# First attention of a fused vision tower: images loaded once, two units beside each other in the row halves

## The reference

```python
patches = img.reshape(B, C, Hp, p, Wp, p).transpose(0, 2, 4, 1, 3, 5).reshape(B, S, C * p * p)
h = einsum('bsk,ek->bse', patches, w) + b            # p = 16, C = 3, k = 768, e = 128
h = h + L0_attn(layernorm(h))    # quantized q, k, v; causal softmax over 196 tokens
h = h + L0_ffn(layernorm(h))     # 8 experts, each takes its best 1024 tokens
h = h + L1_attn(layernorm(h))    # 8 heads, causal
h = h + L1_ffn(layernorm(h))     # 8 experts, two per token
```

## Time and profile before

| | |
|---|---|
| median of 3 runs | 1897.94 us (1896.28 to 1905.5) |
| profiled execution | 1896.8 us, its span 1895.0 us |
| mean granted TensorE clock | 0.929 |
| PE busy | 1663.5 us, 88% of the span |
| PEld busy | 1212.7 us, 64% |
| DVE busy | 1181.9 us, 62% |
| ACT busy | 1075.5 us, 57% |
| POOL busy | 1168.5 us, 62% |
| DMA moved | 172.42 MB, mean 91 GB/s |
| patch products, L449 | 512 matmuls, 207.0 us busy, 511 ns mean |
| copies of pixels | POOL L731 103.8 us, ACT L570 98.6 us |

### The profile page before, as it was taken

How to read it: one execution, slowest core, us unless ns; L and a number is a source line. 1 busy time by engine, 2 the same in 40 slices (tenths; PEclk the granted TensorE clock), 3 DMA queues, 4 the chain that set the end, 5 groups by cost and what they waited for, 6 DMA issues and landing times. The chain is left out here.

```text
span 1895.0 us, 44995 instructions
## 1 busy us (share of the span) xinstructions
PE 1663.5 (88%) x13253; PEld 1212.7 (64%) x13254; DVE 1181.9 (62%) x4868; ACT 1075.5 (57%) x2574; POOL 1168.5 (62%) x1172
## 2 busy tenths in 40 slices
PE   4999999984479873899999999999994999999995
PEld 2666566653456552466666666666662999998985
DVE  2899888883742003588888888888854333444442
ACT  2666666652445432476777777767751555555553
POOL 2455555532068875127767767767666687878876
PEclk8999999995579887699999999999997999999998
DMA  8999999932023334201211111111112454545543
GB/s 199 240 226 231 220 229 228 228 81 61 0 57 68 67 52 95 76 27 47 57 51 53 53 50 53 53 50 52 44 41 66 64 72 66 72 66 69 71 67 38
DMA packets 257798, 172.42 MB, mean 91 GB/s; under 512 B 25598, under 2 KB 250656, under 8 KB 257632
## 3 DMA queue, kind: packets, MB, share of 16 engines
q1 hardware_dynamic: 206432, 134.16, 28.8%
q0 software_dynamic: 50112, 35.64, 13.7%
q10 hardware_dynamic: 1088, 0.53, 0.1%
HBM read 117.64 MB, written 52.40 MB: 90 GB/s over the span
## 5 line engine op out<-in xcount | busy, mean ns | idle before, releaser
L2378 POOL DMA_INDIRECT out_dram<-r_yw,r_idx x212 | 331.0, 1561 | 94.8 <-issue 59.7
L2260 POOL DMA_INDIRECT rows_scratch<-routed_row,slot_u x256 | 252.7, 987 | 169.4 <-DVE slot_u L2199 106.4
L2443 ACT ACTIVATE r_hT<-r_p_up,r_b1T 128x256 f32<-128x256 f32 x424 | 191.4, 473 | 123.8 <-PE r_p_up L2418 120.3
L1925 ACT ACTIVATE a_probsT<-a_p_sc 98x392 f32<-98x392 f32 x384 | 170.4, 500 | 110.8 <-PE a_p_sc L1682 72.3
L2418 PE MATMUL r_p_up<-r_xgT,r_w1e 128*128 128x256 f32 x848 | 222.2, 385 | 9.2 <-DVE r_w1e L2458 8.5
L2406 PEld LDWEIGHTS r_p_y<-w_all,r_hT 128*128 128x128 f32 x1696 | 222.7, 192 | 11.0
L2406 PE MATMUL r_p_y<-w_all,r_hT 128*128 x1696 | 223.4, 275 | 0.0
L449 PE MATMUL p_embed<-pix,w_pix 96*128 96x392 f32 x512 | 207.0, 511 | 3.5 <-ACT pix L570 3.5
L2030 DVE TENSOR_REDUCE a_negmax<-a_p_max 98x2 bf16<-98x392 f32 x256 | 132.3, 558 | 61.6 <-PE a_p_max L1647 61.6
L2418 PEld LDWEIGHTS r_p_up<-r_xgT,r_w1e 128*128 128x128 f32 x848 | 146.2, 192 | 22.7 <-issue 8.3
L723 POOL TENSOR_SCALAR vare<-mv 98x4 f32<-98x4 f32 x64 | 29.9, 468 | 200.6 <-DVE mv L708 174.5
(11 more groups left out here) (378 smaller groups left out, 4091.5 us busy)
## 6 DMA issues: line engine op xcount, KB each, us to landing
img<-in_x_dram SPq DMA_DIRECT2D x192, 196.0 KB, 4.3
img<-in_x_dram SPq DMA_DIRECT2D x192, 189.0 KB, 4.5
r_xg<-rows_scratch SPq DMA_DIRECT2D x106, 130.0 KB
xn_scratch<-xn SPq DMA_DIRECT2D x32, 196.0 KB
h_scratch<-h SPq DMA_DIRECT2D x32, 196.0 KB
h<-h_scratch SPq DMA_DIRECT2D x32, 196.0 KB
h3b<-h_scratch SPq DMA_DIRECT2D x32, 196.0 KB
out_dram<-h SPq DMA_DIRECT2D x32, 196.0 KB
```

Source lines behind the costliest of these rows:

```text
L1925: act.activation(probsT[:, u % 2, i, :], p_sc[i % 2][:, 0:2 * PAIR], ACT.Exp).then_inc(exped, 1)
L2260: pool.indirect_dma_start(rows_dram, bass.IndirectOffsetOnAxis(ap=slot_u[:, u % ROWS, c, t:t + 1], axis=0), row[:, u % ROWS, c, t, :], Non ...
L2378: pool.indirect_dma_start(acc_dram, bass.IndirectOffsetOnAxis(ap=idx[:, (k - 3) % 4, t:t + 1], axis=0), yw[:, (k - 3) % 4, t, :], None, co ...
L2443: act.activation(hT[:, (k - 1) % 2, f, :], p_up[f][:, 0:G], ACT.Silu, bias=b1T[:, bass.ds(e * FC + f, 1)]).then_inc(act_h, 1)
```

## The change

Each image is loaded once, and two units (a pair q: units 2q and 2q+1) lie in one buffer of `img`: unit 2q in rows 0 to 47, unit 2q+1 in rows 64 to 111. `pix` has 128 rows in the same way. The 16 columns of a patch no longer fit the rows by shifting; a unit has 12 products of 64 rows instead of 8 of 96. Rows 0 to 47 of a half hold column j of products 0 to 11; the 16 rows behind them hold columns 12 to 15: POOL copies these to `pix_side` (four copies), and SP moves them by DMA, channel by channel and half by half (6 transfers of 16 x 1568 numbers per pair), into rows 48 to 63 and 112 to 127 of `pix`, four slots for each channel. Rows 48 to 63 of `img` are filled once with any image (`fill_between`).

PE embeds a unit in two iterations: in iteration n the slots 6 to 11 of unit n and 0 to 5 of unit n+1, in turn, in six "ticks" of two products. The two products of a tick lie in different halves of the rows and write two banks, `p_embed[0]` and `p_embed[1]`. For the bank, `p_ptr` shrinks to one: five blocks of transposed probabilities stand there and the sixth in `p_mm`, and ACT copies `probsT` in three parts. ACT copies columns 0 to 3 of a pair in one iteration and 4 to 7 in the next; POOL copies 12 to 15, then 8 to 11.

The pipeline begins three iterations earlier. SP's first block holds the weights, two fills and 12 loads for pair 0, and the same for pair 1. Stores of `xn2` and `h2` are at unit n-5, logits at n-6, and the two stores share a semaphore.

```diff
-        img = S("img", [2 * rows, 2, 2, GRID * SIDE])
-        pix = S("pix", [2 * rows, 2, half, COLS])
+        img = S("img", [LANES, 2, 2, GRID * SIDE])
+        pix = S("pix", [128, 2, SLOTS, COLS])
+        side = S("pix_side", [LANES, 2, MORE, COLS])
...
-        p_embed = P("p_embed", [128, 512])
+        p_embed = [P(f"p_embed{i}", [128, 512]) for i in range(2)]
...
-        p_ptr = [P(f"p_ptr{i}", [TILE, 512]) for i in range(2)]
+        p_ptr = P("p_ptr", [TILE, 512])
...
+        def load_images(sp, q):
+
+            for h in range(2):
+                for m in range(2):
+                    for c in range(CHANNELS):
+                        at = HALF * h + PATCH * c
+                        dst = img[at:at + PATCH, q % 2, m, :].rearrange("r (g w) -> r g w", g=GRID)
+                        sp.dma_start(dst, imgs[2 * (2 * q + h) + m, c]).then_inc(img_loaded[q % 2], 16)
...
                 load_weights(sp)
-                load_images(sp, 0, 0)
+                fill_between(sp, 0)
+                load_images(sp, 0)
+                fill_between(sp, 1)
+                load_images(sp, 1)
...
-                for j in range(half):
+                for j in range(SLOTS):
                     dve.wait_ge(w_mm, 4 + j)
-                    dve.tensor_copy(w_pix[:, j, :], p_score[j % 2][0:2 * rows, 0:128]).then_inc(w_copied, 1)
+                    for h in range(2):
+                        last = dve.tensor_copy(w_pix[HALF * h:HALF * (h + 1), j, :], p_score[j % 2][0:HALF, 0:128])
+                    last.then_inc(w_copied, 1)
...
+            def move_side(q, channels):
+
+                for c in channels:
+                    for h in range(2):
+                        sp.dma_start(pix[HALF * h + rows:HALF * (h + 1), q % 2, MORE * c:MORE * (c + 1), :],
+                                     side[HALF * h + PATCH * c:HALF * h + PATCH * (c + 1), q % 2]
+                                     ).then_inc(side_in[min(c, 1)][q % 2], 16)
+
             def emit(n, k):
-
-                if live(n, 0, UNITS) and not (isinstance(n, int) and n == 0):
-                    wait(sp, pix_ready, 2 * (n - 1), apart=True)
-                    wait(sp, pix_ready_pool, half // 2 * (n - 1))
-                    load_images(sp, n, k)
+                part, q = part_of(n)
+                if part == "first" and 2 <= q + 1 < PAIRS:
+                    sp.wait_ge(pix_ready, ACT_PER * q)
+                    sp.wait_ge(pix_ready_pool, POOL_PER * q)
+                    load_images(sp, q + 1)
...
+                if 0 <= q < PAIRS and part == "first":
+                    sp.wait_ge(pix_ready, ACT_PER * q + 2)
+                    sp.wait_ge(pix_ready_pool, POOL_PER * q + MORE)
+                    move_side(q, [0])
+                if 0 <= q < PAIRS and part == "second":
+                    sp.wait_ge(pix_ready, ACT_PER * (q + 1))
+                    sp.wait_ge(pix_ready_pool, POOL_PER * (q + 1))
+                    wait(sp, embedded, 2 * q - 2)
+                    move_side(q, [1, 2])
...
+            def patch(n, k, ticks):
+
+                for tick in ticks:
+                    for u, slot in ((n, TICKS + tick), (n + 1, tick)):
+                        if not 0 <= u < UNITS:
+                            continue
+                        q, h = u // 2, u % 2
+                        if slot == 0:
+                            wait(pe, hT_ready, u - 1)
+                        if slot < 2 * MORE:
+                            wait(pe, pix_ready, ACT_PER * q + slot // 2 + 1)
+                        else:
+                            wait(pe, pix_ready_pool, POOL_PER * q + slot - MORE + 1)
+                        if slot < MORE:
+                            wait(pe, side_in[0][q % 2], 32 * (q // 2 + 1))
+                        else:
+                            wait(pe, side_in[1][q % 2], 64 * (q // 2 + 1))
+                        at = slice(HALF * h, HALF * (h + 1))
+                        last = pe.matmul(p_embed[h][:, 0:COLS], w_pix[at, slot, :], pix[at, q % 2, slot, :],
+                                         start=(slot == 0), stop=(slot == SLOTS - 1))
+                        if slot == SLOTS - 1:
+                            last.then_inc(embedded, 1)
```

More of the change, by code:

```diff
@@ L437, in emit_pe @@
         def emit_pe(pe):
-            def patch(n, k, js):
-                if not live(n, 0, UNITS):
-                    return
-                if 0 in js:
-                    wait(pe, pix_ready, 2 * n + 1)
-                    wait(pe, hT_ready, n)
-                if 2 in js:
-                    wait(pe, pix_ready, 2 * n + 2)
-                for j in js:
-                    if j >= half // 2:
-                        wait(pe, pix_ready_pool, half // 2 * n + j - half // 2 + 1)
-                    last = pe.matmul(p_embed[:, 0:COLS], w_pix[:, j, :],
-                                     pix[:, k % 2, j, :], start=(j == 0), stop=(j == half - 1))
-                if half - 1 in js:
-                    last.then_inc(embedded, 1)
+            def patch(n, k, ticks):
[19 more added lines that the diff above has]
+                            last.then_inc(embedded, 1)
             def turn(dst, src):
@@ L529, in emit @@
                     last.then_inc(mixed, 1)
[L530 removed]
+                patch(n, k, [4])
                 if live(n, 3, UNITS):
@@ L553, in emit, with image_there, pixels @@
                     last.then_inc(routed, 1)
[L554 removed]
+            iterations(emit, DEPTH)
         def by_column(k, js):
             return img[:, k % 2].rearrange("r m (q j) -> r j (m q)", j=PATCH)[:, js, :]
[L559 to L562 removed]
+        def image_there(eng, q, done_units):
+            eng.wait_ge(img_loaded[q % 2], 16 * (2 + (q // 2 + 1) * IMG_LOADS))
+            wait(eng, embedded, done_units)
         def emit_act(act):
[L565 to L566 removed]
+            def pixels(n, place):
+                part, q = part_of(n)
+                if not 0 <= q < PAIRS:
                     return
[L568 to L570 removed]
+                if place == 0:
+                    image_there(act, q, 2 * q - 3 if part == "first" else 2 * q - 2)
+                first = 2 * place + (MORE if part == "second" else 0)
+                act.copy(pix[0:LANES, q % 2, first:first + 2, :], by_column(q, slice(first, first + 2))
+                         ).then_inc(pix_ready, 1)
             def exps(n, k, m):
@@ L726, in emit @@
                                            ).then_inc(ready, 1)
-                if live(ahead, 0, UNITS):
-                    image_there(pool, ahead, k_ahead)
-                    for j in range(half // 2, half):
-                        js = slice(j, j + 1)
-                        pool.tensor_copy(pix[:, k_ahead % 2, js, :], by_column(k_ahead, js)).then_inc(pix_ready_pool, 1)
+                part, q = part_of(n)
+                if 0 <= q < PAIRS:
+                    image_there(pool, q, 2 * q - 3 if part == "first" else 2 * q - 2)
+                    if part == "first":
+                        wait(pool, side_in[0][q % 2], 32 * (q // 2))
+                        wait(pool, side_in[1][q % 2], 64 * (q // 2))
+                    for j in range(MORE):
+                        if part == "first":
+                            dst, js = side[:, q % 2, j:j + 1, :], slice(SLOTS + j, SLOTS + j + 1)
+                        else:
+                            js = slice(2 * MORE + j, 2 * MORE + j + 1)
+                            dst = pix[0:LANES, q % 2, js, :]
+                        pool.tensor_copy(dst, by_column(q, js)).then_inc(pix_ready_pool, 1)
                 if ahead == 8:
```

137 lines of the change are left out of this document (70 added, 67 removed).

## The result

| | before | after |
|---|---|---|
| median of the runs beside each other | 1897.39 us (4 runs) | 2060.41 us (4 runs) |
| ratio, with its 95% interval | | 1.0851 (1.083 to 1.0871) |
| profiled span | 1895.0 us | 2056.6 us |
| first and last hT copy | 30.1, 414.7 us | 67.7, 575.1 us |
| from the last hT copy to the end of the span | 1480.3 us | 1481.5 us |

The change costs 163 us, and the last line says where: behind the last hT both kernels take the same time. Everything was lost in the first attention, 37.6 us before the first hT and 123 us between the first and the last.

A forecast was written before the change was run, and what follows sets the result against it. PE's program-order loop through hT was taken as the bound, with DVE's 11.2 us as floor. Patch products +4.2 and start +2.3 gave 6.5 on 1896.8, so 1903.3; the median lies 1.1 higher: 1904, range 1878 to 1915.

The forecast's parts named there:

- The patch products, +0.15 us per unit: PE's loop: six ticks with switching costs replace eight products, period 12.31 for 12.19; +4.2 us over 28 iterations.
- Rivals 1: PE's ticks: no price for switching with 64 rows, hT at 11.5 us, total 1881; chance 0.25 for this side.
- 3 (products one behind the other): PE's ticks: the two halves don't overlap, each tick two passes longer, 3.9 us per unit, about 2010; chance 0.04.
- rival 4: First attention: the change does nothing, PE is not in the loop, period stays 12.19, about 1899; chance 0.06.
- As nothing waits for images in the steady part, this is worth 0: DMA, steady part: 12 loads per pair instead of 24, plus six moves, gain 0; at most 3.3 us.
- DMA should fall from 227 to about 155 GB/s with no effect: Sign in the new trace: 2.4 MB of images, 0.6 of moves and 0.8 of stores in two periods.
- Stores move two iterations up in SP's program, yet SP reaches them at the same point behind the loads. Zero: SP's queue: the earlier place of the stores in the program costs 0 us.
- The start, +2.3 us: Before the steady loop: first product near 32 us, hT of units 0 and 1 near 43 and 48.8; 0 to +6.
- Rival 2: Start: first transfers at 192 GB/s, moves late, first product near 36.5, start costs about 9 us, total 1911; chance 0.15.
- ACT and POOL copy the same 392 columns as often, with more rows: Pixel copies on ACT and POOL: listed among the effects on engines other than PE, with nothing added to the time.

The follow-up runs named there:

- in_order_full: in_order with POOL's vare and rstd operations of both norms over 128 rows in place of 98, the added rows filled once: ratio 1.0085 to the kernel before.
- stores_first: The changed kernel, rows as it has them, with SP issuing the stores and logits ahead of the twelve loads: ratio 1.0352 to the kernel before.
- in_order: Changed kernel with rows 4r + c, loads alternating halves, copies over 127 rows, SP order stores, logits, moves, loads, pair 1's loads behind pair 0's first moves: 1.0498.
- after_128: The changed kernel with img and pix_side of 128 rows and pixel copies over 128 rows in place of 112: ratio 1.109 to the kernel before.
- before_packed: The kernel before with the 16 rows of each image load side by side instead of 6 apart: ratio 1.0729 to the kernel before.
- spread: The changed kernel with channel c's patch row p in row 3p + c of a half instead of 16c + p: ratio 1.0699 to the kernel before.
- ahead: Changed kernel with rows 3r + c, copies over 112 rows, loads alternating halves, loads of pair q + 2 behind the last moves of pair q: ratio 1.0477.
- in_order_112: ahead with SP's order stores, logits, moves, loads; rows 3r + c, copies over 112 rows, rstd over 98: ratio 1.0396 to the kernel before.

## Why the prediction was wrong

Forecast 1904, range 1878 to 1915; measured 2060. By its own steps:

- **The patch products, +0.15 us per unit: right.** A tick starts (0.17 us behind the transposes), passes (0.43 for the first pass) and leaves (0.42) as read from the strip pairs; the period without disturbance is 12.3 for a forecast 12.31. Rivals 1 (11.5) and 3 (products one behind the other) are refuted, and rival 4 (no change) by the result. When placement, queue and POOL's rows are repaired, the loop takes 382.8 us from the first to the last hT, against 384.6 before, where the start held unit 1 back.
- **"As nothing waits for images in the steady part, this is worth 0": the step that failed.** It was put at nothing, and with the stores behind it came to 123 us between the first and the last hT. I took the 238 GB/s of the earlier trace rows as what DMA gives, and asked only whether there were fewer bytes. The diff also moved each load from 16 rows six apart to 16 adjacent ones, and that doubled the packet time, from 61 to 128 ns. "DMA should fall from 227 to about 155 GB/s with no effect" is met to the digit in in_order_full (155), the run in which a load has two rows in a class again; in the changed kernel it was 114 at a share of 0.84. In the earlier trace rows the share of 0.96 to 1.10 was a warning: a resource that is full can't be costed at nothing when its pattern of access changes.
- **"Stores move two iterations up in SP's program, yet SP reaches them at the same point behind the loads. Zero": wrong in the same way.** The point in the queue was right, the cover was not priced: behind 2.4 MB at 238 GB/s stores are 10 us late, which an iteration of 12.2 hides; at 115 GB/s they are 20 us late. stores_first wins 95 us of the 163 by order alone; with fast loads the same order wins nothing (1.0478 against 1.0456, both with xn held; with xn free the place of the loads was worth 0.6%, 1.0158 and 1.0095), so these 95 us are mostly the price of slow loads, and not a second loss beside them.
- **The start, +2.3 us: wrong by 35.** hT of unit 1 was forecast near 48.8 and came at 83.5. SP was through at 36.6 for a forecast 21.9: pair 1's loads were issued 1.7 us apart and not 0.65, which is 118 GB/s, about the rate at which they landed. Rival 2 had the mechanism (late start and late moves) with a rate of 192 GB/s and 1911 us; the first 20 us ran at 126. With the rate repaired and pair 1's loads put behind the first moves (in_order_full) the first product starts at 26.43, before the forecast 32, but hT of unit 0 comes at 47.4, as the moves of the other side rows stand behind twelve loads and PE waits for them until 38.48.
- **"ACT and POOL copy the same 392 columns as often, with more rows": right at 112 rows, by luck.** 127 rows cost 4.1% in in_order, and 128 rows 2.4% in after_128. That POOL's copies hold DVE off can be seen in before, in *rounded* (608 ns); that more rows would move the hold to xn can't.
- **The range was too narrow** because every case in it took the DMA rate as given.

What remains in in_order_full is 15.5 us up to the last hT, of which some 12 stand already at the fourth hT (82.0 against 70.12) and 3.6 are 28 periods of 0.13. So the change as meant, fewer image bytes and passes side by side, has nothing to win here: in PE's order the switching costs what the fewer passes save, and DMA was not the bound (before waits 0.3 us for a DMA between 100 and 400 us).

## What to carry to other kernels

When a diff changes which rows a DMA lands on, cost the DMA anew, even if it moves fewer bytes: count how many rows of one transfer fall into one class (four adjacent rows and the four that lie 32 further on). What stands behind large loads in one queue inherits their time; look at who waits for the buffers of the small stores. And when an instruction takes longer with nothing changed in it, look at what the neighbour on the shared port has queued next, and over how many rows.

## What the runs showed of the hardware

- Loads of 16 rows moved 0.98 MB in 8 us with four rows in a class (before_packed) and 1.68 with two (before); stride 4 within one half was as good as stride 6 over both (66 and 61 ns a packet).
- Loads that alternate between the halves in one queue ran 16% faster than those in groups of six per half (1.97 and 1.70 MB in 8 us).
- POOL's copies over 127 rows behind instructions of 98 rows held DVE's xn at 934 ns in the mean; with the same instructions over 128 rows it took 341. Over 112 rows they never did (xn at 340 ns in after, stores_first, spread, ahead and in_order_112).
- Pairs of 64-row products start 0.01 us apart, and two places fewer in which such pairs stand between full-row work saved 0.37 us of a 12.32 us period.
- After 8.35 us without work PE went on at a granted clock of 0.50, from 397 to 401 us, and a pair of products took 1.68 us instead of 0.93.
